# An attention and mixture-of-experts layer on one core: token pages in two sets, packed weights for known pages, and scatters and gathers placed in TensorE's sequence

## The chip, the core and the metric

The kernel runs on one core of a Trainium2 chip. A core has five engines that run their own instruction streams and meet at semaphores: TensorE (PE) multiplies matrices into eight PSUM banks, VectorE (DVE) and ScalarE (ACT) work on tiles, GpSimd (Pool) does small operations and issues the indirect DMAs, SyncE (SP) issues most other DMAs. Sixteen DMA engines move the data. The metric is the device time of one execution in microseconds, the median of the runs.

## What is computed

The layer takes x of 16 sequences of 512 tokens of 128 numbers. The reference, cut to what matters:

```
h = layernorm(x) * (1 + ca) + sa
q, k, v = split(h @ qkv_w.T + qkv_b);  q, k = rope(q), rope(k)      # 16 heads of 8
attn = softmax(causal(q k^T / sqrt(8)));  x = x + ga * (attn v @ proj_w.T + proj_b)
h = layernorm(x) * (1 + cb) + sb
probs = sigmoid(h @ router_w.T + expert_bias);  top_w, top_idx = top_k(probs, 8)   # of 160
top_w = 2.5 * top_w / sum(top_w)
routed = sum over the 8 experts of top_w * (silu(h @ w_gate[e].T) @ w_down[e].T)   # 128 -> 64 -> 128
shared = silu(h @ w_gate_shared.T) @ w_down_shared.T
x = x + gb * (routed + shared)
```

## The kernel before

The work has two stages. The first goes through the sequences in turns; turn_a(i) merges several streams of steps, each with a start and an end as a share of the turn, and merge sorts all steps of all engines by these places. In turn i stand: core(i), the maxima of the scores of sequence i+1 and the exponentials and products of sequence i; pre(i+2), the norm, the projections and rope, with q and k split into three bf16 parts and stored to DRAM (k_stacks, q_stacks); post, the output projection, second norm, routing and page placement of sequence i-1 (its first HALF = 17 steps) and of i-2 (the rest); and scatters. Every engine runs its own steps of the merged list in order.

A token goes to 8 experts. Its row of h2 is copied to 8 rows of a DRAM tensor, pages. A page has 128 rows and belongs to one expert. The first 160 pages belong to experts 0 to 159; when an expert's page is full, post gives it the next free one (page_op, a row of 160 counts on DVE), so the owner of page 160 and up is known only at run time. post writes the last page number of each expert after each sequence to DRAM (ends_store). scatter (L769) is one indirect DMA of 128 rows from Pool; a sequence has 4 x 8 = 32. h2 and pos_s are single buffers: back_keep (ACT, L1044) and keep (DVE, L1050) of a sequence wait until all scatters of the one before have landed (s_scat). SHARE = 18 scatters of a sequence stand in one turn, 14 in the next.

After the last turn come, in this order, post of sequence 15 beside the scatters of sequence 14; the scatters of 15; then table beside shared. table reads the page ends back (L1235), counts with DVE over 6 columns of 2560 numbers how many ends lie at or below each page number (L1240), and so gets each page's owner; the owners go to DRAM and back into a row that SP reads (L1261, L1264). shared is the shared expert of all sequences (up L1135, down L1160, both TensorE).

The second stage, experts, goes through all 672 pages as 168 groups of GRP = 4 pages. b_load (SP) reads four owners into registers for each of four groups and issues for each page one DMA of the expert's weights, 128 rows of 192 numbers (L1286), and rows_in (L1293) one load of 4 pages. The buffers hold DEEP = 8 groups. b_step(G) on TensorE is: down of group G-2 (L1345), gate of group G-1 (L1329), transposes of group G (L1310); DVE copies the transposed rows (L1318, from group SWITCH = 56 on ACT, L1321), ACT does silu (L1337), DVE and ACT copy the results, and ACT stores 256 KB of results (L1300). The weights' buffer w_in and the page buffer x_in are views of prob, which holds the exponentials in the first stage.

gathers (Pool, L1392) fetches the results: one indirect DMA for each token tile and rank, 64 x 8 = 512. Those of sequence n wait until 48 + 8n groups are stored. combine (DVE, L1402 to L1409) multiplies 8 ranks by their weights, adds them, and adds the residual; put (SP, L1415) stores the output. In SP's order put stands between the group loads, from group PUTS = 68 on one every 3.5 groups. Pool's buffer holds TILES = 8 tiles.

## Time and profile before

| | us |
|---|---|
| median of 3 runs | 2200.42 |
| lowest, highest | 2197.68, 2208.45 |
| the profiled execution, its own time | 2189.18 |
| its span | 2187.3 |
| attention products end | 1267.6 |
| first group's transpose | 1369.05 |
| first gather, last gather | 1518.06, 2179.05 |

The span is the time from the first to the last instruction of the profiled execution; all places in time are microseconds from its start. Busy times and clocks are of that execution alone. The mean granted clock of TensorE is 0.746 of full speed. "Idle before, releaser" of a row is how long the engine waited and for what.

### The profile page before, as it was taken

The page shows a single profiled execution, that of the slowest core. Times are in us where ns is not written, and L with a number is a line of the kernel's source. Part 1 is how long each engine was busy: PE and PEld are TensorE (multiplying, and loading weights), DVE is VectorE, ACT ScalarE, POOL GpSimd, SP SyncE. Part 2 cuts the span into 40 slices and gives each one's busy share as a digit, 9 for nine tenths or more (in the row PEclk, how much of TensorE's full clock was granted, in tenths as well). Part 3 has the DMA queues.
Part 4 walks back from the last instruction along what each step waited for, and adds up shares of the span by engine and source line. Part 5 has one row for each costly group of instructions (what it writes and reads, how often), then busy time and mean ns, then how long its engine had stood idle before and what let it go on. Part 6 is the DMA issues. An engine that isn't in the chain of part 4 may idle for free.

```text
span 2187.3 us, 33316 instructions
## 1 busy us (share of the span) xinstructions
PE 1379.2 (63%) x10342; PEld 692.4 (32%) x10342; DVE 1190.1 (54%) x4186; ACT 757.6 (35%) x1599; POOL 1147.3 (52%) x1190
## 2 busy tenths in 40 slices
PE   3568887877787787778778743877776777600000
PEld 1123333323332332333333311555454555400000
DVE  3657766677677676666767436433333333434333
ACT  0045444434444443344345411222544544400000
POOL 1101255555555554555465666001777777777776
PEclk9579778777877787777778856888878877755555
DMA  4594445454444445444444313999999999812211
GB/s 137 174 292 133 138 133 146 127 174 127 134 144 137 134 140 155 135 133 139 138 134 128 105 64 96 293 301 297 351 330 321 344 327 327 290 57 59 60 57 54
DMA packets 291644, 380.99 MB, mean 174 GB/s; under 512 B 46457, under 2 KB 175627, under 8 KB 291340
## 3 DMA queue, kind: packets, MB, share of 16 engines
q1 hardware_dynamic: 234508, 267.65, 40.7%
q0 software_dynamic: 32768, 67.17, 9.9%
q10 hardware_dynamic: 24192, 44.05, 5.4%
q8 instruction: 83, 1.36, 0.2%
q14 instruction: 93, 0.76, 0.1%
HBM read 218.52 MB, written 160.18 MB: 173 GB/s over the span
## 4 chain that ended last, share of the span: by engine, by line
PE 25%; POOL 21%; DVE 19%; DMA 12%; issue 10%; SPq 10%; ACT 2%; POOLq 0%; DVEq 0%; ACTq 0%
POOL vh L1392 17%; DVE masked L554 7%; SPq L1286 4%; PE bank L544 4%; DMA prob<-pages 4%; PE bank L693 4%; DMA km<-k_stacks 4%; SPq L479 3%; PE bank L424 3%; POOL pages L769 2%; DMA k_stacks<-k_part 2%; PE bank L630 2%; PE bank L868 2%; PE bank L490 1%; DMA pages<-h,pos_s 1%
## 5 line engine op out<-in xcount | busy, mean ns | idle before, releaser
L1392 POOL DMA_INDIRECT vh<-results,pos_all x512 | 506.1, 988 | 316.0 <-DMA results<-v_ext 161.3
L554 DVE CUSTOM_DVE_ANT_0 masked<-bank,cb_all 128x512 bf16<-128x512 f32 (+3 forms) x1024 | 444.6, 485 | 280.2 <-PE bank L544 277.9
L769 POOL DMA_INDIRECT pages<-h,pos_s x512 | 504.8, 986 | 165.0 <-issue 164.6
L657 ACT ACTIVATE prob<-bank 128x512 f32<-128x512 f32 x640 | 347.5, 597 | 410.7 <-PE bank L642 406.4
L544 PE MATMUL bank<-km,qm 64*128 64x512 bf16 (+3 forms) x1024 | 210.4, 361 | 171.3 <-DVE rmax L554 106.7
L1402 DVE TENSOR_TENSOR vh<-vh,wts_all 128x1024 f32<-128x1024 f32 x64 | 79.2, 1238 | 406.1 <-DMA vh<-results,pos_all 406.1
L693 PE MATMUL bank<-prob,v_ext 128*32 128x512 f32 (+3 forms) x2048 | 234.2, 539 | 2.0 <-ACT prob L657 2.0
L1310 PE MATMUL bank<-c_all,prob 128*128 128x128 f32 x672 | 135.1, 334 | 148.9 <-DMA prob<-pages 148.0
L630 PE MATMUL bank<-qe,ke 64*128 64x512 bf16 (+3 forms) x1024 | 161.1, 346 | 36.5 <-ACT prob L657 33.0
L544 PEld LDWEIGHTS bank<-km,qm 64*128 64x128 bf16 x1024 | 50.3, 99 | 333.3 <-DVE rmax L554 194.6
L1310 PEld LDWEIGHTS bank<-c_all,prob 128*128 128x128 f32 x672 | 86.7, 165 | 192.0 <-DMA prob<-pages 179.3
L1345 PE MATMUL bank<-prob,ke 64*128 64x128 f32 x1344 | 146.4, 346 | 0.5 <-ACT ke L1337 0.5
L1329 PE MATMUL bank<-qe,prob 128*64 128x128 f32 x1344 | 132.8, 328 | 9.7 <-DVE qe L1318 0.8
L1359 ACT ACTIVATE v_ext<-bank 128x256 f32<-128x256 f32 x280 | 95.3, 382 | 120.7 <-PE bank L1345 114.8
L1405 DVE TENSOR_REDUCE oT<-vh 128x128 f32<-128x1024 f32 x64 | 121.3, 1895 | 2.2
L458 POOL TENSOR_TENSOR rest<-full,q_part 128x512 f32<-128x512 f32 x16 | 18.4, 1153 | 196.3 <-ACT q_part L452 196.3
L1345 PEld LDWEIGHTS bank<-prob,ke 64*128 64x128 f32 x1344 | 109.1, 227 | 37.2 <-issue 29.8
L1321 ACT ACTIVATE qe<-bank 128x512 f32<-128x512 f32 x112 | 66.9, 597 | 143.9 <-PE bank L1310 140.6
L630 PEld LDWEIGHTS bank<-qe,ke 64*128 64x128 bf16 x1024 | 46.6, 97 | 188.5 <-issue 124.3
L642 PE MATMUL bank<-cb_all 64*128 64x128 bf16 (+1 forms) x1280 | 102.2, 227 | 0.0
L1318 DVE COPY qe<-bank 128x512 f32<-128x512 f32 x56 | 38.7, 691 | 110.8 <-PE bank L1310 110.8
L1329 PEld LDWEIGHTS bank<-qe,prob 128*64 128x64 f32 x1344 | 85.1, 160 | 43.5 <-DVE qe L1318 15.4
(187 smaller groups left out, 1850.8 us busy)
## 6 DMA issues: line engine op xcount, KB each, us to landing
prob<-wexp SPq DMA_DIRECT2D x672, 96.0 KB
pages<-free_rows SPq DMA_DIRECT2D x42, 1024.0 KB, 7.5
prob<-pages SPq DMA_DIRECT2D x168, 256.0 KB
results<-v_ext ACTq DMA_DIRECT2D x168, 256.0 KB
qm<-q_stacks SPq DMA_DIRECT2D x64, 256.0 KB, 3.4
km<-k_stacks SPq DMA_DIRECT2D x64, 256.0 KB, 4.7
qe<-q_stacks SPq DMA_DIRECT2D x64, 256.0 KB, 3.8
ke<-k_stacks SPq DMA_DIRECT2D x64, 256.0 KB, 4.5
```

Source lines behind the costliest of these rows:

```text
L544: last = e.matmul(MX[g % 2][:, c0:c0 + (i + 1) * P], qm[rows_, c % 2, h, i * P:(i + 1) * P], km[rows_, c % 2, h, 0:(i + 1) * P], start=Tru ...
L554: last = e.tensor_tensor_reduce(out=masked[:, g % 2, c0:c0 + (i + 1) * P], in0=MX[g % 2][:, c0:c0 + (i + 1) * P], in1=mask_w[:, S - (i + 1 ...
L630: e.matmul(ST[g % 3][:, c0:c0 + S - j * P], ke[rows_, c % 2, h, j * P:(j + 1) * P], qe[rows_, c % 2, h, j * P:S], start=(k == 0), stop=Tru ...
L642: return e.matmul(out_, pick[rows_, :], over, start=False, stop=True, skip_group_check=True)
L657: e.activation(prob[:, slot, :], ST[g % 3][:, :], ACT.Exp, scale=SCALE).then_inc(s_exa, 1)
L693: last = e.matmul(PV[32 * g:32 * g + 32, j * P:S], v_ext[:, j, 4 * c + g, :], prob[:, (c % 2) * UNITS + u, c0:c0 + S - j * P], start=(j == ...
L769: e.indirect_dma_start(out=pages, in_=h2[:, t, :], in_offset=None, out_offset=bass.IndirectOffsetOnAxis(ap=pos_s[:, t * TOPK + k:t * TOPK ...
L1310: last = e.transpose(TX[G % 2][:, :].rearrange("d (p q) -> d q p", q=GRP)[:, q, :], x_in[:, G % DEEP, q, :], ident)
L1329: last = e.matmul(GT[G % 2][half:half + 64, (j // 2) * P:(j // 2 + 1) * P], w_in[:, G % DEEP, j, 0:INTER], x_T[G % 2][:, j * P:(j + 1) * P ...
L1345: last = e.matmul(YP[G % 2][j % 2][:, (j // 2) * D:(j // 2 + 1) * D], h_g[G % 2][half:half + 64, (j // 2) * P:(j // 2 + 1) * P], w_in[half ...
L1392: e.indirect_dma_start(out=y8[:, i, k, :], out_offset=None, in_=results[0:ready * 4 * GRP * P, :], in_offset=bass.IndirectOffsetOnAxis(ap= ...
L1405: sum_d.done(e.tensor_reduce(o_sb[:, i, :], y8[:, i, :, :].rearrange("p k d -> p d k"), AX.X, ALU.add), "sum")
```

## The change

It touches five things.

The pages come in two sets. Set 1 takes sequences 0 to 13 (LATE = 14): 160 known pages and 448 others, groups 0 to 151, NPAGE1 = 608. Set 2 takes sequences 14 and 15: again 160 known pages and 64 others, groups 152 to 207. There are 832 pages and 208 groups. restart sets the page row back at sequence 14. There are 52 clears of 1 MB (clear) instead of 42. ready in gathers is now 48 + 8n groups for n below 14, 200 and 208 for the last two.

Known groups (entry(G) is None: 0 to 39 and 152 to 191) take their weights from wpack, one DMA of 128 rows of 512 numbers for four experts, with no owner from a table.

table exists twice. table(0) counts 4 columns of 2240 numbers in turn 15, table(1) one column of 320 after group 58; SP stores and reads the second before group 80.

tail() replaces what stood between the last turn and experts. It merges post(15), the scatters of sequence 14 and 15, shared, and the steps of groups 0 to 29. The first 30 groups use one set of PSUM banks in place of two. The page loads of set 1 wait for the scatters of sequences 0 to 13, those of set 2 for all.

Scatters and gathers wait for a place in TensorE's sequence: paced for those of the turns (a count of exponential or maximum products, two pairs before the scatter's own place), beside for the last two sequences (a count of transposed groups, s_T), and in gathers a wait on s_Y for every second one.

```
+LATE = 14
+NPAGE1 = NE + LATE * SPAN
+NPAGE = 2 * NE + NB * SPAN
+PACK = GRP * INTER + GRP * D // 2
-PUTS = 68
+PUTS = 64
...
+            def restart(e):
+                D_.wait(e, "open", n - 1)
+                e.wait_ge(s_ends, 16 * n)
+                e.memset(fill[:, :], 0.0).then_inc(s_new, 1)
+                e.memset(endp[:, then, :], float(NPAGE1 + NE)).then_inc(s_new, 1)
...
+        def paced(steps, i, start, end):
+
+            def step(e, f, at):
+                pairs, part = divmod(int(4 * UNITS * at) - 2, 2)
+                if pairs >= 0 and (part == 1 or i + 1 >= NB):
+                    wait(e, s_exp, 4 * UNITS * i - UNITS + 2 * (pairs + 1))
+                elif pairs >= 0:
+                    e.wait_ge(s_mxp, 4 * UNITS * (i + 1) + 2 * (pairs + 1))
+                f(e)
...
-            if 3 <= i <= NB:
+            if 3 <= i < NB:
+                streams.append(paced(scatters(i - 3)[SHARE:], i, 0.0, 0.4))
+            if i == NB:
                 streams.append((scatters(i - 3)[SHARE:], 0.0, 0.44))
             if 2 <= i < NB:
-                streams.append((scatters(i - 2)[:SHARE], 0.54, 0.99))
+                streams.append(paced(scatters(i - 2)[:SHARE], i, 0.52, 0.98))
...
+                if at is None:
+                    first = (G if G < NGRP1 else G - NGRP1) * P
+                    e.dma_start(w_flat[:, G % DEEP, 0:PACK], wpack[first:first + P, :]).then_inc(s_wl[G % DEEP], 16)
...
+            if G == NGRP1:
+                e.wait_ge(s_scat, 16 * NT * TOPK * NB)
...
+                    if k % 2 == 0:
+                        e.wait_ge(s_Y, min(NGRP, NE // GRP + (T * TOPK + k) // 3))
...
-                    while PUTS + 7 * stored // 2 < 4 * (k + 1):
+                    while PUTS + 13 * stored // 4 < 4 * (k + 1) and stored < NB * NT:
...
+        def beside(steps, first):
+
+            def step(e, f, groups):
+                wait(e, s_T, groups)
+                f(e)
+            return [{"pool": lambda e, f=st["pool"], g=first + 13 * k // len(steps): step(e, f, g)}
+                    for k, st in enumerate(steps)]
+
+        def tail():
+            sh = shared()
+            return merge((post(NB - 1), 0.0, 0.62, 0.6), (beside(scatters(NB - 2), 0), 0.0, 0.55), (beside(scatters(NB - 1), 15), 0.63, 1.0),
+                         (sh[:-2], 0.04, 0.85), (sh[-2:], 0.86, 0.98),
+                         ([b_step(G) for G in range(EARLY)], 0.02, 1.0, 0.0))
...
-                run(name, e, merge((post(NB - 1), 0.0, 1.0, 0.6), (scatters(NB - 2), 0.0, 0.8)))
-                run(name, e, scatters(NB - 1))
-                run(name, e, merge((table, 0.0, 0.3), (shared(), 0.0, 1.0)))
+                run(name, e, tail())
```

Where the order moves. On Pool, in the middle of a turn, before the change: L769 are scatters, L458 is the second part's rest of q, L1063 to L1070 compute the token weights of post.

```order
L769 DMA pages<-h,pos_s 86016x128 x10
L458 TENSOR_TENSOR rest<-full,q_part 128x512 [waits pre_g,pre_a]
L769 DMA pages<-h,pos_s 86016x128
L1063 TENSOR_TENSOR hit<-hit,sg 128x256 [waits post_d]
L1066 TENSOR_TENSOR hit<-hit 128x32x4 [waits post_g]
L1068 TENSOR_TENSOR hit<-hit 128x32x2 [waits post_g]
```

The same place on Pool after it; L784 are scatters, L473 the rest of q, L1092 the token weights.

```order
L784 DMA pages<-h,pos_s 106496x128 [waits s_exp]
L784 DMA pages<-h,pos_s 106496x128 [waits s_mxp]
L784 DMA pages<-h,pos_s 106496x128 [waits s_exp]
L473 TENSOR_TENSOR work<-work,shelf 128x512 [waits pre_g,pre_a]
L1092 TENSOR_TENSOR hit<-hit,sg 128x256 [waits post_d]
```

One scatter moved from behind the rest of q to before it, and scatters that ran one after another now wait for counts of TensorE's products.

On TensorE, behind the last attention product, before the change: L693 is that product, L707 to L811 turn and project it, L847 to L868 are post's norm and router logits.

```order
L693 MATMUL bank<-prob,v_ext 32x256 x3
L707 MATMUL bank<-c_all,oT 128x128 [waits s_ov]
L707 MATMUL bank<-c_all,oT 128x128 x3
L789 MATMUL bank<-c_all,onorm 128x128 [waits post_a,s_on]
L789 MATMUL bank<-c_all,onorm 128x128 x3
L800 MATMUL bank<-on_att,w_all 128x512 [waits post_a]
L811 MATMUL bank<-c_all,on_att 128x128 [waits post_a]
L811 MATMUL bank<-c_all,on_att 128x128 x3
L847 MATMUL bank<-c_all,xn 128x128 [waits post_d]
```

The same place after it: L819 and L830 are post's, L1420, L1442 and L1462 the transposes, gate and down products of the groups, L1178 the shared expert's first product.

```order
L819 MATMUL bank<-on_att,w_all 128x512 [waits post_a]
L1420 MATMUL bank<-c_all,prob 128x128 [waits s_fina,s_xl0]
L1420 MATMUL bank<-c_all,prob 128x128 x3
L830 MATMUL bank<-c_all,on_att 128x128 [waits post_a]
L830 MATMUL bank<-c_all,on_att 128x128 x3
L1178 MATMUL bank<-vh,w_all 64x512 [waits s_tabd1,post_a,s_gba,s_on]
L1178 MATMUL bank<-vh,w_all 64x512
L1442 MATMUL bank<-qe,prob 64x128 [waits s_wl0,s_XT]
L1442 MATMUL bank<-qe,prob 64x128 x3
L1420 MATMUL bank<-c_all,prob 128x128 [waits s_xl1]
```

The transposes of group 0 moved into post of the last sequence, between its projection and its turn back, and wait there for their page load. Sequence 15's positions need products that stand between groups 16 and 18.

## Rows read from the trace of the kernel before

**Rows 1.** The page: busy tenths in 40 equal slices, of Pool and the DMA engines

```profile
POOL 1101255555555554555465666001777777777776
...
DMA  4594445454444445444444313999999999812211
```

**Rows 2.** Stages: length, busy PE, PEld, DVE, ACT, Pool, clock, DMA share, GB/s

```profile
110.00:1190.00 1080.00, 837.36 (x6156) 348.93 (x6152) 748.56 (x3305) 472.14 (x927) 514.56 (x539) 0.77 0.49 147
...
1268.00:1369.00 101.00, 38.22 (x214) 19.64 (x214) 54.01 (x142) 11.14 (x19) 61.35 (x66) 0.58 0.32 89
...
1400.00:1518.00 118.00, 87.60 (x756) 62.48 (x752) 40.84 (x75) 28.82 (x75) 0.00 (x0) 0.84 0.94 295
1518.00:1910.00 392.00, 278.44 (x2339) 198.03 (x2336) 141.10 (x157) 187.30 (x459) 300.99 (x299) 0.82 1.01 330
1910.00:2180.00 270.00, 0.00 (x0) 0.00 (x0) 98.54 (x107) 0.00 (x0) 205.09 (x214) 0.50 0.20 58
...
1274.00:1336.00 62.00, 20.89 (x78) 10.05 (x79) 38.56 (x109) 6.55 (x11) 43.41 (x47) 0.50 0.20 65
```

**Rows 3.** Timeline of Pool, gathers: start, length, count, [idle before, releaser]

```profile
1518.06 0.99 POOL L1392 DMA_INDIRECT vh<-results,pos_all  x1 [160.10 <-DMA results<-v_ext]
...
1559.23 0.94 POOL L1392 DMA_INDIRECT vh<-results,pos_all  x1 [0.32 <-DMA results<-v_ext]
...
2177.80 0.94 POOL L1392 DMA_INDIRECT vh<-results,pos_all  x1 [0.30 <-issue]
2179.05 0.94 POOL L1392 DMA_INDIRECT vh<-results,pos_all  x1 [0.30 <-issue]
```

**Rows 4.** Timeline of TensorE and SP, and (second row) the chain, to group 0

```profile
1263.47 4.10 PE L693 MATMUL bank<-prob,v_ext 128*32 128x512 f32 x32 [1.32 <-ACT prob L657]
...
1315.77 16.89 DVE prob L1240 x12
...
1348.83 17.51 SPq L1286 DMA_DIRECT2D prob<-wexp  x32
1366.39 3.74 SPq L1293 DMA_DIRECT2D prob<-pages  x8
...
1369.05 1.12 PE L1310 MATMUL bank<-c_all,prob 128*128 128x128 f32 x4 [18.27 <-DMA prob<-pages]
```

**Rows 5.** Timeline of TensorE: transposes of neighbouring groups, at two clocks

```profile
1372.01 1.12 PE L1310 MATMUL bank<-c_all,prob 128*128 128x128 f32 x4
...
1375.26 1.12 PE L1310 MATMUL bank<-c_all,prob 128*128 128x128 f32 x4
...
1385.86 0.66 PE L1310 MATMUL bank<-c_all,prob 128*128 128x128 f32 x4
...
1387.89 0.66 PE L1310 MATMUL bank<-c_all,prob 128*128 128x128 f32 x4
```

**Rows 6.** DMA queues and issues, 1380 to 1510 us (first three), 1550 to 1900

```profile
q1 hardware_dynamic: 29704, 27.05, 69.6%
q10 hardware_dynamic: 6614, 12.04, 24.9%
...
results<-v_ext ACTq DMA_DIRECT2D x45, 256.0 KB
...
q0 software_dynamic: 8507, 17.44, 17.1%
...
vh<-results,pos_all POOLq DMA_INDIRECT x266
```

**Rows 7.** Waits: in one turn, in all of 218 to 1130 us, at the attention's end

```profile
626.28 1.15 POOL L458 TENSOR_TENSOR rest<-full,q_part 128x512 f32<-128x512 f32 x1 [8.94 <-ACT q_part L452]
...
ACT h L1044 <- DMA pages<-h,pos_s: 19.9, 11, 2.4
...
DVE pos_s L1050 <- DMA pages<-h,pos_s: 14.1, 11, 1.9
...
1261.33 0.60 PE L630 MATMUL bank<-qe,ke 64*128 64x256 bf16 x3 [8.41 <-ACT prob L657]
```

280 lines of the change are left out of this document (182 added, 98 removed).

## The prediction

> **What bounds the kernel now.** I read the two strips of the page first [rows 1]. In the last six of the 40 slices (of 54.7 us) the DMA engines fall from 9 tenths to 2, while Pool stays at 7. The other dip in the DMA strip stands just before slice 25, where Pool still works and nothing streams. The table of stages puts numbers on both [rows 2]: from 1268 to 1369 us, between the last attention product and the first expert group, the DMA engines are 0.32 busy at a granted clock of 0.58; from 1910 to 2180 us TensorE does nothing and Pool issues gathers.
>
> So the end of the kernel is one engine in a row. Pool issues the first gather of results at 1518.06, the last at 2179.05 [rows 3]: 511 steps in 661.0 us, 1.29 us each. Until 1910 it makes 299 in 392 us, 1.31 each, beside full DMA queues [rows 2]; after that 1.25. The expert groups are done 270 us before Pool is. Neither the matmuls nor the bytes of the groups set the end: the moment of the first gather does. That moment is a chain [rows 4]: the attention products end at 1267.6; post of the last sequence and its 32 scatters; DVE counts page ends for the table until 1333; the table goes out and back; SP issues 32 weight loads from 1348.8 and the first page loads at 1366.4; TensorE transposes the first group at 1369.05; 48 groups must be stored before gather 0, which is 149.0 us after the first transpose.
>
> **The change part by part.**
>
> *The early start of the groups.* Groups 0 to 39 now hold known experts, need no table, and read pages that scatters of sequences 0 to 13 filled. Those scatters land at about 1260 in the trace, before the last product, since TensorE waited 8.4 us for them there [rows 7]. SP's gate is then the end of the attention products, which hold the weights' buffer. Behind it: eight packed loads where 32 single ones took 17.51 us, so 4.4 us, and eight page loads. The eight packed loads are 2.1 MB; the page load behind them lands with them, at the 330 GB/s of the full stage [rows 2] about 6.5 us, and 2.7 us was the distance from page issue to transpose. I take 9 us behind the last product: first transpose at 1276.6 instead of 1369.05, **92 us earlier**. If page load and issue add up it is 12 us.
>
> *What lies beside the first 30 groups.* Post of sequence 15, both last runs of scatters and the shared expert now stand between these groups on every engine; a group waits where they wait. On TensorE a group with its data there takes 2.03 us at the full clock of 2.4 GHz and 3.25 us at 1.2 GHz [rows 5]. The rest of the work is the 38.2 us that TensorE was busy in the stage 1268 to 1369 at clock 0.58 [rows 2], so 22 at full clock and 44 at half. Ends: 30 x 2.03 + 22 = 83 us, 30 x 3.25 + 44 = 142 us. For the clock I take 0.80, near the 0.82 to 0.84 of the stages where groups stream: 76 + 28 = 104, and 4 for waits on DVE and ScalarE: **108 us**. Other engines are shorter: Pool's 64 scatters at a gather's 1.3 are 83 us, and the DMA time comes to 79. The last needs the price of a packed group. In 130 us without gathers the queues of SP (q1) and ScalarE (q10) were busy 69.6% and 24.9% for 45 groups: 2.73 us of queue time a group, one group in 2.89 us [rows 6]; a 256 KB store of results is 0.72 of it, the page load of the same size I take as the same, so 384 KB of single weights are 1.29. Packed they are 256 KB in rows as long as those of a page: 0.72, and a packed group 2.16 us. 64 scatters at 0.22, a gather's price (q0, 17.1% of 350 us for 266), are 14.
>
> *Groups 30 to 47.* Ten packed groups at 2.2 and eight others at 2.9 are 45 us. The way from the last transpose to the stored result is 149.0 less 47 x 2.89, 13 us. First transpose to first gather: 108 + 45 + 13 = **166 us, 17 more than before**. So the first gather comes 75 us earlier, at about 1443. Pool must be free by then: the last scatters start when sequence 15's positions are ready, beside group 17 or 18, near 1341, and need 42 us. That is the cover, with some 60 us to spare.
>
> *The gathers.* The same 512. Their new wait on the count of groups asks for 40 groups plus one for three gathers; 120 groups took the 392 us of the stage, 3.3 each, in which Pool makes 2.5 gathers, so the wait is met unless a group takes over 3.9 us. A met wait is nearly free: the gather behind a row of five waits came after 0.32 us instead of 0.30 [rows 3], so at most 5 us in all; I take 0. Forty groups are added. From group 48 on there are 40 packed and 120 others. With 2.5 gathers beside each (0.57) and stores of the output the others keep 3.3, the packed ones take about 2.8: 113 + 400 = 513 us, so the groups end near 1950. Until then gathers run at 1.316, 385 of them, and the other 126 at 1.25: 665 us, **4 more**. The second set's last 64 gathers need groups 200 and 208: Pool comes to them at 1443 + 448 x 1.31 = 2030, long after.
>
> Here a page speaks for another split. The row first: next to DVE's two-input products of the combination, in the last 220 us, a gather still takes 1.25 us; the longer step stands where the DMA queues are full [rows 2, 3]. The Trainium skill, page "GPSIMD Engine Reference", section "8. Key points", says that GpSimd shares its SBUF interfaces with VectorE and contends with instructions that have two SBUF inputs. By that rule the step would go with DVE's work, which is the same beside each gather in both kernels, and the gathers would stay at 661 us; by the rows they are 665.
>
> *The turns.* One scatter of each turn stood behind the q rest on Pool, which waited 8.9 us for ScalarE; its DMA then held DVE's pos_s and ScalarE's h. In 11 turns those waits are 14.1 and 19.9 us [rows 7]. Now all go ahead of the rest operation. I take DVE's 14 as the gain. Against it: each scatter waits on a pair of exp products two pairs back. In turn 15 this stretches the first 18 scatters of sequence 13 to the last exp pairs, about 3 us later than Pool had them, and these scatters end in TensorE's 8.4 us wait. Net **11 us earlier**, between 26 (20 plus TensorE's own idle) and 10 the other way. Ten more clears of 1 MB lie in turns whose DMA engines are 0.49 busy [rows 2]; uncovered each would cost 3 us. The first table's count, some 11 us of DVE in turn 15, lies in a stretch where post of sequence 14 waits for Pool anyway; without that cover it costs up to 11 us. The second table stalls SP about 15 us near group 80 (the way from the end of the count to the first weight load in [rows 4]), which the eight-group buffer and Pool's lag hide. Zeroing and restart of the page row in turn 14 are three operations of a row of 160, under 1 us.
>
> *Sum.* Span 2187.3 - 92.5 + 17 + 4 - 11 = 2105 us. The profiled execution was 2189.18 us, 1.9 over its span and 11.2 under the median 2200.42. So 2107, and for the median of runs **2118 us**, 3.7% faster.
>
> **The rivals.**
>
> *The tail stays at 1.2 GHz.* In the trace the clock was 0.50 from 1274 to 1336, with TensorE busy a third of the time [rows 2]. If waits of post hold the groups so often that it stays low, the 108 us are 142: 2152. For it: every engine takes its instructions in order, and DVE puts blocks of up to 1.4 us (two additions) ahead of a copy. Against: in [rows 5] the clock was full 12 us after the first group, as groups came one upon another.
>
> *All goes well.* Full clock in the tail (83) and 20 us from the turns: 2118 - 25 - 9 = 2084.
>
> *The placing of scatters does nothing, or a little harm, in the turns.* The hit, rstd and k operations stay the late ones, and the chain runs through DVE's reductions anyway: 0 to +10 us in place of -11: 2129 to 2139.
>
> *The groups become the bound.* 208 groups would have to end after Pool reaches gather 480, near 2070: 160 groups in 625 us, 3.9 us each against 3.3. If so the end is their end plus 32 gathers, 40 us, and the time about 2140.
>
> *Slower than before.* A paced scatter at the head of Pool's queue holds the k rest and its third part behind it; those feed the stores and loads that the next turn's first products wait for. If TensorE's exp pair is itself late, the wait goes round. Without the turns' 11 the forecast gains 71.5 us, so each of 13 turns would have to lose 5.5 us to use it up; a loss of 8 us a turn, about the 8.9 us that one such wait took, gives 2129 + 104 = 2233. Against: each wait asks for pairs that stand two pairs before the scatter's own place in TensorE's sequence.
>
> **How the numbers follow.** Forecast (2102 to 2137) 0.55; low clock in the tail 0.16; all well 0.10; turns without gain 0.09; groups the bound 0.05; slower 0.05. The range of 8 in 10 goes from 2083 to 2157: below it lies a little of the good case, above it a few cases of low clock together with turns without gain, and the slower rival. About 0.5% is what a measurement of this kernel can tell from no change, 11 us; between 2189 and 2211 I leave 0.01, above 0.04, and the rest is faster.
>
> **What would show it.** Right: first transpose of a page 8 to 13 us behind the last attention product; first gather between 1418 and 1462, last one 660 to 670 us behind it; groups over well before Pool; in the turns no wait of pos_s on a scatter. Wrong: over 3.9 us per group beside gathers, gathers waiting for results at the second set, a clock of 0.5 through the first 30 groups, or the attention products ending later than 1268.

## The result and the profile after

The changed kernel takes 2122.18 us, the median of four runs (2113.71 to 2127.52), where the kernel before takes 2199.97 (median of four too). The ratio is 0.9647, with a 95% interval of 0.9615 to 0.9679. Its profiled execution took 2120.34 us with a span of 2118.5.

The strips of the page of the changed kernel, one digit for each fortieth of the span, answer to [rows 1]:

```profile
POOL 1011155455545545545554565325777777777776
PEclk9988777767767677777777768998877878997555
DMA  4585445544545454554544226799999999997121
```

The low stretch of the DMA strip ahead of the experts is now two slices wide where it was three, and it lies before the end of attention. The two slices behind it have TensorE's clock at 8 and 9. Further on Pool still makes its row of sevens, and the DMA engines still fall before Pool does, three slices from the end where it was five: the end of the kernel is the same engine in a row, begun sooner.

The stages, as in [rows 2] (window, length, busy PE, PEld, DVE, ACT, Pool, granted clock, DMA share, GB/s):

```profile
1284.00:1397.00 113.00, 89.15 (x858) 61.59 (x858) 65.66 (x170) 35.05 (x82) 61.61 (x66) 0.94 0.76 251
1397.00:1444.00 47.00, 38.86 (x380) 27.77 (x378) 22.87 (x43) 14.50 (x39) 0.00 (x0) 0.93 0.96 318
1560.00:1760.00 200.00, 146.05 (x1168) 104.21 (x1168) 70.95 (x76) 95.24 (x234) 153.64 (x153) 0.78 1.01 327
1760.00:1938.00 178.00, 136.25 (x1302) 95.79 (x1300) 63.52 (x68) 101.30 (x261) 136.72 (x136) 0.93 1.04 364
```

In the first of them TensorE is busy 89 of 113 us at a granted clock of 0.94. The stage that it replaces in [rows 2] had it busy 38 of 101 us at 0.58.

Timeline of TensorE, the places that answer to [rows 4] and the last row of [rows 7], and the transposes of group 30:

```profile
1266.42 0.60 PE L645 MATMUL bank<-qe,ke 64*128 64x256 bf16 x3 [5.98 <-ACT prob L672]
...
1268.56 4.50 PE L708 MATMUL bank<-prob,v_ext 128*32 128x512 f32 x32 [1.32 <-ACT prob L672]
...
1283.72 1.12 PE L1420 MATMUL bank<-c_all,prob 128*128 128x128 f32 x4 [5.43 <-DMA prob<-pages]
...
1390.39 0.65 PE L1420 MATMUL bank<-c_all,prob 128*128 128x128 f32 x4
```

The attention products end at 1273.06, 5.5 us later than before. The first transpose stands 10.7 us behind them, the 31st 106.7 us behind the first. Timeline of Pool, the first and the last gather, as in [rows 3]:

```profile
1444.03 0.99 POOL L1512 DMA_INDIRECT vh<-results,pos_all  x1 [47.14 <-DMA results<-v_ext]
...
2110.23 0.94 POOL L1512 DMA_INDIRECT vh<-results,pos_all  x1 [0.31 <-issue]
```

From first transpose to first gather 160.3 us, from first gather to last 666.2. What Pool waited for ahead of its gathers, in us and times:

```profile
  issue: 147.6, 484
  DMA results<-v_ext: 49.3, 8
  PE bank L1462: 5.2, 17
```

All but 2 of the 49.3 us are the wait ahead of the first gather. The new wait on the count of groups (L1462 is the down product that raises it) is the 5.2 us, 17 times. Waits in the eleven steady turns, the window of [rows 7]:

```profile
POOL pages L784 <- PE bank L559: 103.3, 72, 4.6
...
POOL pages L784 <- PE bank L657: 59.6, 55, 7.7
```

The last number is the longest. The two rows of [rows 7] in which VectorE and ScalarE waited for a scatter to land are gone from the answer. In their place Pool waits for TensorE ahead of 127 scatters, 163 us in all. In the last two turns they are not gone: from 1155 to 1266 us VectorE's pos_s still waits 8.0 us and ScalarE's h 7.6 us for a scatter to land.

### The profile page after: what moved, and what is told of

It reads as the page before. It is cut to its first block, busy times and chain, and to the rows that moved or that the text cites. A ratio compares the mean times of both kernels' runs of the same rounds, so it can differ in the third digit from the quotient of the medians.

```text
span 2118.5 us, 35198 instructions
## 1 busy us (share of the span) xinstructions
PE 1470.0 (69%) x11142; PEld 748.5 (35%) x11142; DVE 1180.8 (56%) x4183; ACT 817.8 (39%) x1761; POOL 1149.6 (54%) x1190
## 4 chain that ended last, share of the span: by engine, by line
PE 31%; DVE 22%; DMA 16%; POOL 11%; SPq 11%; issue 8%; ACT 2%; POOLq 0%; ACTq 0%; DVEq 0%
POOL vh L1512 9%; DVE shelf L569 8%; DMA prob<-pages 6%; SPq L1392 5%; PE bank L559 4%; PE bank L708 4%; DMA km<-k_stacks 4%; SPq L494 3%; PE bank L439 3%; PE bank L887 2%; PE bank L1420 2%; DMA k_stacks<-shelf 2%; PE bank L645 2%; PE bank L1442 2%; DMA results<-v_ext 1%
## 5 line engine op out<-in xcount | busy, mean ns | idle before, releaser
L784 POOL DMA_INDIRECT pages<-h,pos_s x512 | 502.0, 980 | 324.5 <-issue 115.0
L569 DVE CUSTOM_DVE_ANT_0 shelf<-bank,cb_all 128x512 bf16<-128x512 f32 (+3 forms) x1024 | 444.8, 486 | 283.8 <-PE bank L559 281.5
L1420 PE MATMUL bank<-c_all,prob 128*128 128x128 f32 x832 | 158.1, 320 | 130.9 <-DMA prob<-pages 129.5
L1462 PE MATMUL bank<-prob,ke 64*128 64x128 f32 x1664 | 171.9, 332 | 15.4 <-ACT ke L1450 14.5
L1476 ACT ACTIVATE v_ext<-bank 128x256 f32<-128x256 f32 x360 | 121.6, 381 | 150.9 <-PE bank L1462 106.7
L1420 PEld LDWEIGHTS bank<-c_all,prob 128*128 128x128 f32 x832 | 101.1, 158 | 182.7 <-DMA prob<-pages 165.2
L1442 PE MATMUL bank<-qe,prob 128*64 128x128 f32 x1664 | 157.9, 318 | 8.5 <-DVE qe L1428 1.5
L1431 ACT ACTIVATE qe<-bank 128x512 f32<-128x512 f32 x152 | 91.1, 599 | 161.8 <-PE bank L1420 161.3
L1462 PEld LDWEIGHTS bank<-prob,ke 64*128 64x128 f32 x1664 | 128.3, 216 | 63.5 <-issue 31.9
L1442 PEld LDWEIGHTS bank<-qe,prob 128*64 128x64 f32 x1664 | 100.6, 154 | 47.2 <-ACT qe L1431 19.3
L473 POOL TENSOR_TENSOR work<-work,shelf 128x512 f32<-128x512 f32 x32 | 37.1, 1158 | 145.8 <-ACT shelf L467 145.6
L657 PE MATMUL bank<-cb_all 64*128 64x128 bf16 (+1 forms) x1280 | 104.4, 233 | 0.0
L1450 ACT ACTIVATE ke<-bank 128x256 f32<-128x256 f32 x208 | 80.1, 385 | 45.6 <-PE bank L1442 42.4
```

The source lines that it names most:

```text
L569: last = e.tensor_tensor_reduce(out=masked[:, g % 2, c0:c0 + (i + 1) * P], in0=MX[g % 2][:, c0:c0 + (i + 1) * P], in1=mask_w[:, S - (i + 1 ...
L784: e.indirect_dma_start(out=pages, in_=h2[:, t, :], in_offset=None, out_offset=bass.IndirectOffsetOnAxis(ap=pos_s[:, t * TOPK + k:t * TOPK ...
L1420: last = e.transpose(TX[G % 2][:, :].rearrange("d (p q) -> d q p", q=GRP)[:, q, :], x_in[:, G % DEEP, q, :], ident)
L1442: last = e.matmul(gt(G)[half:half + 64, (j // 2) * P:(j // 2 + 1) * P], w_gate(G, j), x_T[G % 2][:, j * P:(j + 1) * P], start=True, stop=True)
L1462: last = e.matmul(yp(G)[j % 2][:, (j // 2) * D:(j // 2 + 1) * D], h_g[G % 2][half:half + 64, (j // 2) * P:(j // 2 + 1) * P], w_down(G, j), ...
L1476: e.activation(dst, src, ACT.Identity).then_inc(s_mine, 1)
```

## The experiments

The turns are timed by one operation that stands in each once, the first product of post's token weights on Pool (L1092; L1063 in the kernel before), through its start. "Steady turn" is the mean of the ten from the second to the twelfth such row, "last three" the sum of the three behind them. Places are us from the start of the profiled span. The letters name the chips (which one ran the first result is not on record, so a may be one of the others); the first two rows are the kernels of the first result.

| kernel | chip | median us | ratio to before (95%) | steady turn | last three | attention ends | first transpose | first gather |
|---|---|---|---|---|---|---|---|---|
| before | a | 2199.97 | | 75.8 | 172.5 | 1267.6 | 1369.1 | 1518.1 |
| changed | a | 2122.18 | 0.9647 (0.9615 to 0.9679) | 75.1 | 183.1 | 1273.1 | 1283.7 | 1444.0 |
| g1_after_again | d | 2114.50 | 0.9643 (0.9615 to 0.9670) | 74.8 | 181.8 | 1270.1 | 1280.4 | 1440.7 |
| e5_single_w | d | 2136.41 | 0.9728 (0.9695 to 0.9761) | 75.1 | 182.2 | 1271.6 | 1290.5 | 1464.3 |
| h1_unpaced_sequential | e | 2161.69 | 0.9856 (0.9824 to 0.9888) | 75.4 | 172.6 | 1265.6 | 1360.2 | 1476.3 |
| h2_table_early | e | 2124.81 | 0.9689 (0.9662 to 0.9715) | 74.5 | 176.6 | 1261.2 | 1266.5 | 1441.8 |
| e1_turns_unpaced | b | 2508.35 | 0.9643 (0.9588 to 0.9699) | 84.6 | 239.8 | 1432.0 | 1442.3 | 1639.9 |
| e2_place_only | b | 2497.73 | 0.9581 (0.9529 to 0.9634) | 83.7 | 241.1 | 1427.0 | 1436.8 | 1631.1 |
| e3_table_tail | b | 2388.33 | 0.9191 (0.9122 to 0.9259) | 76.4 | 196.0 | 1299.1 | 1309.6 | 1515.5 |
| e4_before_paced | b | 2483.23 | 0.9519 (0.9455 to 0.9584) | 77.7 | 200.6 | 1319.1 | 1435.7 | 1586.9 |
| f1_turns_unpaced | c | 2511.66 | 0.9695 (0.9665 to 0.9725) | 85.0 | 237.8 | 1434.8 | 1445.8 | 1643.6 |
| f2_before_paced | c | 2469.44 | 0.9531 (0.9504 to 0.9558) | 77.4 | 196.8 | 1312.8 | 1428.2 | 1574.9 |
| e6_no_merge | c | 2413.98 | 0.9292 (0.9228 to 0.9355) | 76.6 | 201.9 | 1308.6 | 1427.8 | 1540.5 |
| e9_best | c | 2393.86 | 0.9266 (0.9206 to 0.9326) | 76.7 | 211.7 | 1318.9 | 1324.8 | 1524.9 |

The kernel before took 2606 and 2595 us on chips b and c, 2195 and 2194 on d and e. The chips b and c are told of at the end of this section; what follows on the change's terms rests on d and e, whose kernel before agrees with that of chip a.

### The same kernel again

No edit.

> The changed kernel itself, unaltered, on the chips of the experiments. There the kernel before takes 2606 and 2595 us instead of 2200, TensorE pauses for up to 28 us with nothing that the profile names to release it, and a ratio to the kernel before can only be read beside this one. The kernels with GpSimd's waits in the turns ended attention at 1299 to 1319 us, those without at 1432 to 1435 us. My theory: the waits make that difference, so this kernel ends attention near 1300 to 1320 us and takes 2380 to 2400 us, a ratio of 0.92, and the pauses come beside GpSimd's indirect DMAs. Rival: the kernels differ for another reason (the table's place in turn 15, or their code alone), and this one ends attention at 1430 us with a total of 2500 us, a ratio of 0.96.

On this chip the kernel before took 2195.14, and the ratio is that of the first result to four parts in ten thousand. The terms repeat as well: 10.3 us from attention to the first transpose, 160.3 to the first gather, 662.0 to the last. The pauses of chips b and c are absent, so neither theory about them was decided by this run. What it gives is the distance of two profiles of the same kernel: 3 us in the end of attention, 0.0 us in the way from first transpose to first gather, and 4.2 us in the gathers.

### Packed weights undone

```
 def b_load(e, k):
...
-                    e.dma_start(w_flat[:, G % DEEP, 0:PACK], wpack[first:first + P, :]).then_inc(s_wl[G % DEEP], 16)
+                    for j in range(GRP):
+                        e.dma_start(w_in[:, G % DEEP, j, :], wexp[(GRP * (first // P) + j) * P:...]).then_inc(s_wl[G % DEEP], 16)
```

> The changed kernel, but every known group loads its weights as four DMAs from the experts' own places, as the other groups do, not as one DMA from the packed array: the packing is undone, the two sets, the overlap and the pacing stay. 80 groups load 4 times 96 KB instead of 256 KB, so 240 more DMAs on SP's queue and 128 KB more each. In the change's trace a group cost 3.25 us beside post and scatters, and SP's four issues 1.9 us. My theory: TensorE sets the pace of these groups and SP's issues are beside it, so that it costs little: 0 to 10 us over the changed kernel. Rival: the loads are what sets the first 48 groups' pace (DMA share 0.96 in the stage from group 30 to 47), and 32 of these groups at 0.5 us more each add 15 us or more ahead of the first gather, and as many in the gathers if these need the groups: over 15 us in all.

The median is 21.9 us above that of the changed kernel on the same chip, which is what the rival had said. The profile says where. First transpose of this kernel, timeline of TensorE:

```profile
1290.51 1.12 PE L1421 MATMUL bank<-c_all,prob 128*128 128x128 f32 x4 [12.59 <-DMA prob<-pages]
```

It waits 12.6 us for its page load, where the changed kernel waited 3.9 here (5.4 in the first result), and stands 19.0 us behind the attention products, not 10.3. These 8.7 us are the 32 single loads that stand ahead of that page load on SP; the other 1.4 of the 10.1 us between the two first transposes are attention, which ended later. From the first transpose to the first gather it is 173.8 us instead of 160.3, 13.5 more for 40 groups. The gathers took 665.0 us instead of 662.0. Those three (10.1, 13.5, 3.0) are 26.6 us, the difference of the two spans (26.5).

That the loads made the 13.5 us, as the rival had it, is shown for a part only. Groups 0 to 29 and 30 to 46 of the changed kernel (g1_after_again), then of this one, as in [rows 2]:

```profile
1280.40:1388.80 108.40, 86.21 (x796) 58.84 (x796) 61.48 (x162) 32.72 (x75) 58.66 (x63) 0.92 0.76 241
1388.80:1426.00 37.20, 32.36 (x345) 23.23 (x342) 21.64 (x42) 12.83 (x35) 2.87 (x3) 1.00 1.00 347
```

```profile
1290.50:1406.50 116.00, 92.52 (x796) 63.33 (x796) 61.52 (x162) 32.72 (x75) 58.73 (x63) 0.84 0.79 256
1406.50:1451.00 44.50, 36.40 (x345) 25.96 (x341) 21.80 (x42) 12.85 (x34) 2.88 (x3) 0.88 0.96 320
```

TensorE's waits for page loads from group 30 to the first gather, in the same order:

```profile
PE bank L1420 <- DMA prob<-pages: 2.7, 1, 2.7
```

```profile
PE bank L1421 <- DMA prob<-pages: 7.2, 6, 2.2
```

In the first 30 groups, 7.6 us longer here, TensorE waits for no load behind the first in either kernel; it is busy 6.3 us longer for the same products, at a granted clock of 0.84 instead of 0.92. In the groups behind them it waits 4.5 us more for page loads and is busy 4 us longer, at 0.88 instead of 1.00. Why the clock was lower no row says, and one profile of this kernel can't tell an effect of the loads from chance. So the packing is worth 22 us between attention and the first gather (8.7 and 13.5), of which 13 are traced to loads, and 3 behind it, which is less than the 4.2 us between the changed kernel's own two profiles.

### Unpaced turns, and groups behind the rest

```
-                streams.append(paced(scatters(i - 3)[SHARE:], i, 0.0, 0.4))
+                streams.append((scatters(i - 3)[SHARE:], 0.0, 0.44))
-                streams.append(paced(scatters(i - 2)[:SHARE], i, 0.52, 0.98))
+                streams.append((scatters(i - 2)[:SHARE], 0.54, 0.99))
...
 def tail():
+            return merge((post(NB - 1), 0.0, 1.0, 0.6), (scatters(NB - 2), 0.0, 0.8)) + scatters(NB - 1) \
+                + shared() + [b_step(G) for G in range(EARLY)]
```

> The changed kernel with two parts undone in stages that don't touch. In the turns the scatters stand at the places of the kernel before, without GpSimd's waits. Behind attention TensorE does the rest of the last query tile, its scatters and the shared expert first and then the groups, none beside them; two sets, packed weights and table stay. The changed kernel on the last chip has steady turns of 75.0 us, its last three add to 181.8 us (172.5 in the kernel before), attention ends at 1270, the first transposes stand at 1280, the first gather at 1441. On a chip where the kernel before takes 2200 my theory for the turns: steady 75.9 us, last three 173 us, attention ends within 3 us of 1270. Rival: the last three stay at 182 us, and attention ends at 1279. For the overlap, theory: first transposes 101 us behind attention as in the kernel before (1371), then 48 groups in 115 to 125 us instead of 160, so the first gather comes 45 to 55 us later and the total is 2160 to 2170. Rival: the loads hold the groups as they did, first gather 80 us later, total 2195, no gain over the kernel before at all; or the overlap is worth little, as on the pausing chips (first gather 216 us behind attention there with the overlap, 232 us without), total 2130.

*The turns.* The last three are 172.6 us, as in the kernel before, and attention ends 4.5 us earlier than in the changed kernel. Timeline of Pool, the rows behind these numbers, kernel before and changed kernel:

```profile
1088.46 0.72 POOL L1063 TENSOR_TENSOR hit<-hit,sg 128x256 f32<-128x256 f32 x1 [2.15 <-DVE hit L1059]
...
1260.99 0.72 POOL L1063 TENSOR_TENSOR hit<-hit,sg 128x256 f32<-128x256 f32 x1 [2.15 <-DVE hit L1059]
```

```profile
1082.96 0.72 POOL L1092 TENSOR_TENSOR hit<-hit,sg 128x256 f32<-128x256 f32 x1 [1.98 <-DVE hit L1088]
...
1266.08 0.72 POOL L1092 TENSOR_TENSOR hit<-hit,sg 128x256 f32<-128x256 f32 x1 [2.15 <-DVE hit L1088]
```

and this kernel:

```profile
1086.35 0.72 POOL L1092 TENSOR_TENSOR hit<-hit,sg 128x256 f32<-128x256 f32 x1 [2.15 <-DVE hit L1088]
...
1258.97 0.73 POOL L1092 TENSOR_TENSOR hit<-hit,sg 128x256 f32<-128x256 f32 x1 [2.15 <-DVE hit L1088]
```

The steps of the three turns are 68.5, 54.2, 49.8 in the kernel before; 70.8, 58.0, 54.3 in the changed one; 69.2, 53.5, 49.9 here, with the table's counts still in turn 15. The last turns are short: they have nothing to project, and 50 us is not much more than Pool needs for 32 scatters at 1.26. The chain of the changed kernel there goes through the table's counts (L1310), and then a scatter, released by a product of TensorE for the exponentials (L657), begins the last row of scatters:

```profile
1222.17 2.55 DVE work L1310 x2
...
1225.40 2.46 DVE work L1310 x2
...
1237.31 2.45 DVE work L1310 x2
...
1244.69 0.16 PE bank L657 x3
...
1245.13 0.96 POOL pages L784
...
1261.71 0.96 POOL pages L784
1262.97 2.23 DMA pages<-h,pos_s
1265.28 0.60 ACT h L1073
```

Unpaced, the chain runs through Pool alone from 1221.70 on, one scatter every 1.26 us:

```profile
1221.70 1.03 POOL pages L784
...
1254.60 0.95 POOL pages L784
1255.86 2.23 DMA pages<-h,pos_s
1258.17 0.60 ACT h L1073
```

The last scatter of sequence 13 is landing at 1255.86 instead of 1262.97, ScalarE's h is free 7.1 us earlier, and the attention products end 7.5 us earlier than in the changed kernel's first profile. In the steady turns the paced kernels have 74.5 to 75.1 us, this one 75.4, the kernel before 75.8. So placing and waiting together are worth at most 0.3 to 0.9 us a turn, less in ten turns than the last three lose, and even that is not clear: eight of the ten steps of this kernel are 75.0 to 75.2 us, where the changed one has 74.6 to 75.5, and the surplus stands in two (77.7 and 76.0). The two waits of [rows 7] are back at nearly their old length in the same window:

```profile
ACT h L1073 <- DMA pages<-h,pos_s: 19.3, 11, 1.8
...
DVE pos_s L1079 <- DMA pages<-h,pos_s: 13.5, 11, 1.3
```

So most of their length was not on the path that sets a steady turn.

*The overlap.* The stages of this kernel from attention's end to the first transpose, and from there to the first gather:

```profile
1266.00:1360.00 94.00, 48.30 (x214) 24.88 (x214) 31.57 (x105) 11.28 (x19) 60.85 (x66) 0.51 0.25 88
1360.00:1476.00 116.00, 101.19 (x1036) 72.14 (x1032) 59.94 (x110) 38.39 (x103) 0.00 (x0) 0.97 0.94 330
```

The groups stand 94.6 us behind attention, but once begun they need 116 us for what takes 160 beside post. The way from attention to the first gather is 210.7 us without the overlap, 170.6 with it, and 250.5 in the kernel before. So laying the groups beside the rest is worth 40 of the 80 us. The theory of this run had the total right (2160 to 2170 us) and this step at 45 to 55. The other 40 the sequential tail has too: 7 us because the first transposes stand 94.6 and not 101.5 us behind attention, without the table and with eight packed loads where 32 stood, and 33 because 48 groups are stored in 116.1 instead of 149.0 us. Of these groups 40 are packed, and the first eight had been loaded long before; which of the two gave how much of the 33 us was not taken apart. The median is 1.4% under that of the kernel before, and 47 us over that of the changed kernel on chip d; the profiled spans differ by 37. On chip e the profiled executions of both kernels were 11 to 13 us shorter than their medians, which no row explains.

### The table's counts behind attention, weights one product earlier

```
-                streams.append((table(0), 0.55, 0.9))
...
 def tail():
+            tb = table(0)
+                         ([{"dve": st["dve"]} for st in tb[1:]], 0.25, 0.6), (sh[:-2], 0.04, 0.85),
...
-                e.wait_ge(s_pv, 4 * NB)
+                e.wait_ge(s_pv, 4 * NB - 1)
                 for k in range(DEEP // 4):
                     b_load(e, k)
...
 def b_load(e, k):
+                if G == 6:
+                    e.wait_ge(s_pv, 4 * NB)
```

> The changed kernel with two edits to make it faster. The counts for the table of known pages stand on VectorE behind attention and not in turn 15, and the weights of the first six groups may be loaded one attention product earlier. GpSimd's waits stay in all turns. Theory for the turns: the counts (four of 2.5 us) lie inside the last turn's path, and without them the last three turns add to 176 to 178 us, not 181.8, so attention ends near 1265. If the counts were the whole loss, 172.5 us and 1261; if they are hidden, 181.8 us and 1270. Theory behind attention: on the pausing chip the same edit brought the first transposes from 10 to 5.8 us behind the last attention product, so it gives 4 us. Total 2105 to 2108 where the changed kernel has 2114.5, if the table is still there before the groups that read it (48 on) need it; the rival is that the table comes late or its counts delay the copies of the first groups, and the total is that of the changed kernel or above.

Both edits did what they were for, and the total is that of the rival all the same. The last three turns are 176.6 us: without the counts the third of them is 49.4 instead of 54.3, the other two stay (70.4, 56.8). Attention ends at 1261.2, and the first transpose stands 5.3 us behind it. That is 13.9 us ahead of the changed kernel on chip d. The first gather, though, comes at 1441.8, 1.1 us later, and the median ratio is 0.9689, if anything above 0.9643. The 14 us are given back among the first 30 groups: from the first transpose to the 31st it takes 122.2 us instead of 108.5. TensorE's waits from 1262 to 1441, this kernel and then the changed one again (g1_after_again):

```profile
PE bank L1177 <- DVE xr L1208: 15.2, 7, 3.9
PE bank L1201 <- DVE work L1192: 14.2, 6, 6.9
```

```profile
PE bank L1203 <- DVE work L1194: 9.8, 6, 2.6
PE bank L1178 <- DVE xr L1210: 9.5, 6, 3.0
```

These are the shared expert's two products. TensorE waits 10.1 us longer for VectorE, whose queue now holds the four counts of 2.5 us (10 us) as well; the rest of the 13.7 us is mostly TensorE busy 2.4 us longer, at a granted clock of 0.87 instead of 0.92. SP besides stood for the table in the midst of the packed loads:

```profile
1375.02 0.44 SPq L1324 DMA_DIRECT2D page_table<-table_i  x1
1385.45 0.24 SPq L1333 DMA_DIRECT2D ke<-page_table  x1
1385.79 0.33 SPq L1389 DMA_DIRECT2D prob<-wpack  x1
```

TensorE ran on through these 10 us out of its buffer of eight groups, so they are not shown to cost anything. The counts lie on the path in either place; the place where they would be free was not found.

### Two chips with pauses

The other eight kernels ran on chips b and c. TensorE stops there again and again, and the waits lead back to nothing that the profile can name. Timeline of ScalarE in f1_turns_unpaced, beside the gathers; "remote" is a release that the profile ties to no instruction of the program:

```profile
1734.55 0.66 ACT L1476 ACTIVATE v_ext<-bank 128x256 f32<-128x256 f32 x2 [14.93 <-remote]
1749.31 0.38 ACT L1450 ACTIVATE ke<-bank 128x256 f32<-128x256 f32 x1 [14.10 <-remote]
```

and TensorE at the same place:

```profile
1749.74 1.23 PE L1462 MATMUL bank<-prob,ke 64*128 64x128 f32 x8 [27.91 <-ACT ke L1450]
```

The kernels with waits in Pool's queue and those without part company on these chips.

The scatters at the old places, no waits (the first part of the diff of h1_unpaced_sequential):

> The changed kernel, but the scatters of the turns stand at the places that they had in the kernel before (0.0 to 0.44 and 0.54 to 0.99 of a turn) and GpSimd does not wait on TensorE's place before each. The last scatters behind attention, the groups and the gathers are as changed. My theory: the gain per steady turn (75.87 us before, 75.09 us after, 11 turns, 8.6 us) comes from the placing of the scatters, and the changed kernel loses 11 us between the last km load and the end of the attention products (139.9 us before, 151.0 us after) to the same placing in turn 15. Then here the steady turn is 75.9 us, the last stretch is near 140 us, and attention ends within 3 us of the changed kernel's 1273, so that the whole run is the same to within 4 us. Rival: the loss at the end comes from the counts of the pages' table on VectorE in turn 15, which stay here: then the last stretch stays at 151 us and attention ends 8 us later, a total of some 2130.

> The changed kernel with the scatters of the turns at the places of the kernel before, without GpSimd's waits on TensorE's place. It is the kernel of the first such experiment again, because the four kernels of that group ran with waits of up to 24 us that the profile puts down to nothing in the kernel, and its turns differed by 8 us from run to run. In the change's traces the periods of the turns were 75.9 us before and 75.1 us after in the steady ones, and 68.5, 54.2 and 49.8 us before, 70.8, 58.0 and 54.3 us after, in the last three. My theory: both differences come from the placing and pacing of the scatters, so here the steady turn is 75.9 us, the last three add to 173 us, attention ends within 4 us of the changed kernel's 1273, and the total is 2118 to 2126. Rival: the last three turns lose their 11 us to other parts of the change (the table's counts, the packed clears), stay at 183 us, and with steady turns of 75.9 the total is 2130.

The changed places, no waits (`paced(scatters(i - 3)[SHARE:], i, 0.0, 0.4)` becomes `(scatters(i - 3)[SHARE:], 0.0, 0.4)`, and so the other):

> The changed kernel, its scatters of the turns at the changed places (0.0 to 0.4 and 0.52 to 0.98 of a turn), but without the waits of GpSimd on TensorE's place. My theory: GpSimd runs ahead without the waits, scatters come in bursts that compete with the km loads as before, and the steady turn is 75.9 us as in the kernel before. Rival: the order in GpSimd's queue alone makes the gain, the steady turn stays at 75.1 us, and the run is the same as the changed kernel to within 3 us, or faster by up to 8 us if the waits cost something in turn 15.

The waits, with the table's counts behind attention:

> The changed kernel, but the counts for the table of known pages (VectorE, 2.5 us each) stand behind attention, among the work beside the first groups, and not in turn 15. My theory: they are VectorE's work inside the softmax's path in turn 15, and 4 of the 11 us that the last stretch lost (139.9 us before, 151.0 us after) are theirs; the stretch becomes 147 us, attention ends at 1269, and the first known group that uses the table is read late enough that nothing waits for it: total 2118. If the counts were the whole loss: stretch 140 us, attention end 1262, total 2111. If they are hidden: attention ends at 1273 and the total is that of the changed kernel, 2122.

The kernel before with `paced` and its places, nothing else:

> The kernel before, with one part of the change alone: the scatters of turns 2 to 15 stand at the changed places and wait for TensorE's place. Everything behind attention is as in the kernel before, and there is no table of pages in turn 15. My theory: the steady turn goes from 75.87 to 75.1 us (8.6 us over 11 turns), the early turns, whose clears stay few here, do not lose their 3 us, and the last stretch loses 7 us (140 to 147): attention ends at 1263 instead of 1267.6 and the total falls by some 5 us, to 2195. Rival: the pacing itself costs the whole 11 us at the end, and the total is 2200, unchanged.

> The kernel before with the placing and pacing of the turns' scatters alone, again for the same reason. Theory: steady turns 75.1 us (minus 8.6 us in all), last three turns 183 us instead of 172.5 (plus 10.6 us): total 2198, the same as before. Rival: the last three turns stay at 172.5 us, because their loss is from the table's counts or the clears, and the total is 2191.

The changed kernel with the sequential tail of h1_unpaced_sequential but paced turns:

> The changed kernel, but behind attention TensorE's sequence is as in the kernel before: first the rest of the last query tile and its scatters, then the shared expert, then the groups; the first 30 groups are not laid beside them. The two sets of pages, the packed known weights and the table stay. My theory: the overlap is the whole gain: the first transposes come at 1370 instead of 1284, but then run free of other work, 30 groups in 66 to 75 us instead of 107, so the first gather comes 45 to 55 us later and the total is 2170 to 2180. Rival: the gain is from the packed weights and the two sets, the groups' pace on the DMA queues is what sets the first gather, and the total stays below 2135.

The changed kernel with the edits of h2_table_early, and turn 15 unpaced:

> The changed kernel with three edits to make it faster: the weights and pages of the first six groups may be loaded one attention product earlier (the first transposes wait 5.4 us for them, 10.7 us behind the last attention product), the table's counts stand behind attention, and the scatters of turn 15 are not paced. My theory: the first transposes come 4 us earlier in relation to attention, and attention ends 4 to 7 us earlier: total 2112 to 2115. Rival: the earlier loads take the DMA engines from the last turn's km and ke loads and the table's counts delay the groups beside which they now stand, and the total is that of the changed kernel, 2122, or above.

The three without waits have steady turns of 83.7 to 85.0 us and end attention at 1427 to 1435; the five with waits have 76.4 to 77.7 and end at 1299 to 1319. Places alone do nothing that can be told (e1 and e2 differ by 5 us at the end of attention); the waits are worth 108 to 133 us there, comparing kernels on the same chip, and the kernel before gains 4.7% of its whole time from places and waits, with nothing else changed (f2). One turn may tell: e9, unpaced in turn 15 only, needs 211.7 us for its last three turns, where e3 and e6 need 196 and 202. None of this came out as expected in numbers, since all were worked out for a kernel of 2200 us. f1 and f2 repeat e1 and e4 on chip c, to 3 us of attention's end in one case and 6 in the other.

The loads are a little slower there, but not by such amounts: from issue to landing the median of ke's loads is 5.6 us in f1_turns_unpaced and 4.5 in the changed kernel on chip a, of qe's 4.2 and 3.8. And the pauses are not there from the start: in the first 200 us, ahead of the first scatter, TensorE's idle stretches of over 3 us sum to 45 us in f1_turns_unpaced and in the changed kernel alike. From 220 to 1200 us they sum to 85 us in f1_turns_unpaced, 57 in e6_no_merge (the same chip, with the waits) and 47 in the changed kernel on chip a. That they come with Pool's indirect DMAs is what this comparison suggests; it is not shown. Why the runs on b and c have them and those on a, d and e don't, and what the engines wait for, stays open. Each chip was used at one time only, so it may be the chip or something else that was so at that time. The changed kernel itself did not run on b or c, so its own ratio there is not known; the nearest, e3, has 0.919.

The tail on these chips is bound otherwise as well: in e3 the groups end near 2304, 63 us before the last gather at 2367, and Pool waited 149 us for L1460's products instead of 5. The overlap was worth less there: on chip c it is 208.8 us from attention's end to the first gather with it (f1) and 231.9 without (e6), 23 us where chips d and e had 40.

## Why the prediction came out right

The forecast was 2118 us with a range from 2083 to 2157, and the kernel takes 2122. The steps behind attention hold. The step for the turns failed, and that the total is right within 4 us is in part luck, since an error of the other sign stands in the last step. By its own steps:

- **First transposes.** Expected 9 us behind the last product, measured 10.7 and 10.3, after waits of 5.4 and 3.9 us for the page load. Right to 1.7 us, in the first result.
- **First 30 groups.** Expected 108 us, measured 106.7. The sum is right by two errors that cancel, which is luck: the clock was 0.94 where I took 0.80 (with it my 104 us become 88), and TensorE idled 24 us of 113 where I had 4 for waits; 19 us of waits for VectorE's part of the shared expert are in the rows of chip d above. The rival of the low clock did not come: TensorE was busy 89 of 113 us and was granted 0.94, where in h1_unpaced_sequential, with no groups beside the rest, it was busy 48 of 94 us and was granted 0.51. (In the trace of the kernel before the clock is full 9 us after its first group, not 12.)
- **Groups 30 to 47 and the way to the first gather.** Expected 45 and 13, measured 39.3 to the transposes of group 47 and 14.4 behind. In all 160.3 instead of 166. Pool was free 47 us before the first gather, where I had some 60 to spare.
- **The price of a packed group.** 2.16 us of queue time against 2.73 was worked out from bytes. The undoing cost 13.5 us over 40 groups, 0.34 each, where I had 0.57; it cost another 8.7 us at the first page load, where I had 17.5 less 4.4, 13. The order of size is right, and both stand ahead of the gathers. That it is queue time is shown only for the first page load and the 4.5 us of waits behind group 30; the first 30 groups waited for no load.
- **The gathers.** Expected 665, measured 666.2, 662.0 again. The Trainium skill's rule (page "GPSIMD Engine Reference", section "8. Key points") would have kept 661, and totals 4 us apart can't decide between the two. The steps can: 1.31 us while the DMA engines were full and 1.25 to 1.29 behind, as the rows of before had it, while VectorE was busy 36 to 37% of the time in both stretches. The wait on groups cost under its 5.2 us.
- **Groups over before Pool.** Expected 1950, measured transposes until 1938.
- **The turns.** Expected 11 us earlier, measured 5.5 us later: the term that failed, by 16.5 us. I had two entries. The gain of 14 from the waits of pos_s was to come in the steady turns. Those waits went away, and 0.7 us a turn, 7 or 8 us, is what came. Not even that is shown to be theirs: with both waits back (h1_unpaced_sequential) the steady turns are at most 0.3 to 0.9 us longer. A wait is worth its length only where it lies on the path, and these mostly did not; this is the rival on placing, and its own figure, 0 to 10 us later in place of 11 earlier, is where the measured 5.5 lies. Against the gain I had put 3 us for turn 15. The last three turns lost 10.6: with the waits of Pool undone they lost nothing (172.6), with the table's counts moved away 4.1 (176.6). So 4 us are there with the waits alone, and 5 to 6.5 more appear only when waits and counts are both there. I had named both, the scatters stretched to the last exp pairs and the count that costs up to 11 without its cover, and taken each at its low end. That the waiting scatters used up the count's cover is how I read the two chains.
- **From span to median.** I added 11.2 us, the distance of before's profiled execution from its median. For the changed kernel it was 1.8. This cancels 9.4 of the 16.5 us, by luck: nothing in the forecast said that this distance would shrink.

The deviations of the span are 16.5, 1.7 and 1.2 more and 5.7 less, together 13.7: from 2104.8 they lead to the measured 2118.5. Of the signs of being wrong that I had named, one came: the attention products ended at 1273 and 1270, later than 1268. The size of the gain is thus understood. Its split is less so than the sum makes it look: of the 80 us between attention and first gather, taking the overlap away costs 40 (h1) and taking the packing away 22 (e5). The two need not add up, since the packed groups run at 2.2 us where nothing lies beside them (30 in 65.0 us in h1) and at 3.6 beside post and the shared expert. The other 18 us, and what the missing table and the two sets alone are worth, were not tried.

The slower rival, scatters that hold the rest of k behind them, did not come in the steady turns of any chip: paced ones were shorter everywhere, by little on d and e. Only the last three turns lost.

## What to carry to other kernels

Work laid beside other work is worth less than the stage that it empties: 94 us of a half idle TensorE turned into 40, since the first 30 groups then took 107 us with the rest of the work among them, not 65. A wait in the profile is worth nothing until it is known to lie on the path: the waits of h and pos_s (19.9 and 14.1 us in eleven turns) went away for at most 3 to 9 us in ten. Two small costs that hide under the same slack have to be added before either is called hidden. And a wait that spaces out one engine's indirect DMAs was nearly neutral in the runs on some chips (4.5 us lost at the end of attention) and worth over 100 us on others, so such a wait is judged on more than one chip.

## What the hardware showed that was not expected

- The kernel before took 2200, 2195 and 2194 us in the runs on three chips and 2606 and 2595 on two, each within 1% over its runs. On the slow two the engines paused again and again without a named cause, ScalarE 14 and 15 us in the rows shown and TensorE 28, mostly once scatters or gathers ran.
- On those two, waits in Pool's queue shortened a steady turn of 84 to 85 us to 76.4 to 77.7, and the kernel before from 2595 to 2469 us.
- Undoing the packing (four DMAs of 96 KB rather than one of 256 KB) put the first transposes 8.7 us further behind attention: 32 loads took SP 16.0 us to issue, eight 3.7. The 40 groups took 13.5 us more.
- A round trip of 2 KB through DRAM on SP (the table out, in single 4-byte numbers, and back) kept SP from any other issue for 10.0 us. No loss is shown from it with eight groups in the buffer.
